# Early first slots of the second attention: projections, row writes and first scores moved ahead, first maxima in another bank, ten throwaway matmuls

## The reference

```python
x = x + linear_attention(layernorm(x))   # causal, 16 heads of 8, elu+1 features
x = x + experts(layernorm(x))            # 16 gated experts, top 4 of 16, and 2 shared
x = x + attention(layernorm(x))          # softmax attention, 16 heads of 8, scale 1/sqrt(8)
x = x + experts(layernorm(x))            # the same expert weights
```

## Time and profile before

| | |
|---|---|
| Runs | 553.9, 556.0, 558.52 us; median 556.0 |
| Profiled execution | 559.11 us, of which 557.4 us are the span of the trace |
| Busy over the span | PE 93%, DVE 73%, ACT 61%, POOL 61% |
| Second attention's first scores | 259.01 us |
| Its second chunk's first scores | 290.60 us |
| Mean granted clock of PE | 0.975 of 2.4 GHz |

### The profile page before, as it was taken

How to read it: one execution, slowest core, us unless ns; L and a number is a source line. 1 busy time by engine, 2 the same in 40 slices (tenths; PEclk the granted TensorE clock), 3 DMA queues, 4 the chain that set the end, 5 groups by cost and what they waited for, 6 DMA issues and landing times.

```text
span 557.4 us, 11771 instructions
## 1 busy us (share of the span) xinstructions
PE 520.1 (93%) x3801; PEld 394.2 (71%) x3801; DVE 407.5 (73%) x1098; ACT 340.4 (61%) x606; POOL 337.9 (61%) x429
## 2 busy tenths in 40 slices
PE   7888989998999999998878989898899999999997
PEld 7666556877888888885545656555578888888885
DVE  4678797676787886676787886978278686686564
ACT  3777766665565556555567675656855655555553
POOL 5897683698767877684613042230488685776663
PEclk9999999999999999999699997969999999999999
DMA  7486870732634233347423344110433444364241
GB/s 178 138 268 192 256 226 5 132 115 67 127 121 127 78 133 92 114 130 246 151 80 102 128 133 125 52 36 2 83 110 110 94 140 123 97 142 131 86 146 38
DMA packets 48566, 67.60 MB, mean 121 GB/s; under 512 B 6641, under 2 KB 18946, under 8 KB 48514
## 3 DMA queue, kind: packets, MB, share of 16 engines
q1 hardware_dynamic: 45408, 66.47, 41.1%
q10 hardware_dynamic: 3106, 0.48, 0.5%
HBM read 53.56 MB, written 13.37 MB: 120 GB/s over the span
## 4 chain that ended last, share of the span: by engine, by line
PE 67%; ACT 11%; DVE 7%; POOL 6%; issue 5%; DMA 3%; SPq 1%; POOLq 0%; DVEq 0%; ACTq 0%
PE bank L1006 15%; PE bank L1008 15%; PE bank L1007 15%; ACT PT L885 6%; PE bank L1128 4%; PE bank L1183 4%; PE bank L1160 2%; DVE PT L1571 2%; POOL KS L745 2%; DMA head_rows<-PHI 2%; PE bank L1013 1%; DVE MEXP L1588 1%; PE bank L1107 1%; PE bank L1071 1%; DMA KS<-head_rows 1%
## 5 line engine op out<-in xcount | busy, mean ns | idle before, releaser
L745 POOL TENSOR_TENSOR KS<-PT,QS 128x512 fp32r<-128x512 f32 x143 | 184.6, 1292 | 85.1 <-ACT QS L981 79.5
L976 ACT ACTIVATE bank<-bank 128x512 f32<-128x512 f32 x128 | 74.6, 582 | 103.5 <-PE bank L1008 102.9
L1685 DVE TENSOR_TENSOR PT<-CS,bank 128x512 f32<-128x512 f32 x128 | 87.6, 684 | 57.6 <-PE bank L1008 56.3
L1006 PE MATMUL bank<-XH,WH 128*128 128x512 f32 (+1 forms) x288 | 114.9, 399 | 0.0
L1008 PE MATMUL bank<-XH,WL 128*128 128x512 f32 (+1 forms) x288 | 112.3, 390 | 0.0
L1007 PE MATMUL bank<-XL,WH 128*128 128x512 f32 (+1 forms) x288 | 112.2, 390 | 0.0
L1588 DVE TENSOR_REDUCE MEXP<-bank 128x4 f32<-128x1024 f32 x64 | 78.3, 1224 | 25.4 <-PE bank L1128 24.5
L1690 DVE TENSOR_TENSOR PT<-PT,bank 128x512 f32<-128x512 f32 x128 | 88.0, 688 | 8.3 <-ACT bank L976 0.3
L981 ACT ACTIVATE QS<-PT 128x512 fp32r<-128x512 f32 x144 | 89.9, 624 | 6.2 <-DVE PT L1690 5.9
L885 ACT ACTIVATE PT<-bank 128x1024 f32<-128x1024 f32 x64 | 65.6, 1026 | 41.3 <-PE bank L1160 41.0
L1183 PE MATMUL bank<-PT,V 128*32 128x256 f32 (+1 forms) x1024 | 65.6, 376 | 0.8 <-ACT OTS L899 0.4
(11 more groups left out here) (208 smaller groups left out, 803.9 us busy)
## 6 DMA issues: line engine op xcount, KB each, us to landing
CS<-combine_rows SPq DMA_DIRECT2D x128, 256.0 KB, 3.2
head_rows<-HP SPq DMA_DIRECT2D x28, 256.0 KB, 3.1
QS<-head_rows SPq DMA_DIRECT2D x28, 256.0 KB, 3.0
KS<-head_rows SPq DMA_DIRECT2D x28, 256.0 KB, 3.7
head_rows<-PHI SPq DMA_DIRECT2D x14, 256.0 KB, 3.7
stage<-in_L_ffn_gate_w_dram SPq DMA_DIRECT2D x5, 192.0 KB, 3.9
stage<-in_L_ffn_up_w_dram SPq DMA_DIRECT2D x5, 192.0 KB, 3.9
stage<-in_L_ffn_down_w_dram SPq DMA_DIRECT2D x5, 192.0 KB, 4.5
```

The lines of the kernel that those rows point to most:

```text
L745: pool.tensor_tensor(GL[:, (u - 1) % 3, :], GG[:, (u - 1) % 3, :], GH[:, (u - 1) % 3, :].bitcast(f32), ALU.subtract).then_inc(F.gl, 1)
L976: act.activation(TH[:, u, :] if u < SHARED else G[u % 3][:, :], G[u % 3][:, :], ACT.Silu).then_inc(F.th, 1)
L1006: pe.matmul(out, wh, vh, start=start, stop=False)
L1685: dve.tensor_tensor(ab, CS[:, e % CBUFS, :], U[u % 3][:, :], ALU.mult).then_inc(F.b, 1)
```

## The change

- **Projections of chunk 0** move from units 6 and 8 to units 0 and 2 of the last chunk of the first expert layer, their ACT copies from units 7 and 9 to 1 and 3, POOL's low halves from 8 and 10 to 2 and 4. The values product stays in unit 10. New waits guard bank 7.
- **Row writes of chunk 0** move on SP from behind the last `CS` load to between the loads 5 to 9 of that chunk, and the read of group 0 behind load 11. Groups 1 to 3 stay behind the last load.
- **Late units**: the downs of units 15 and 16 move from ahead of slot 2 to ahead of slot 3, that of unit 17 from slot 3 to slot 4, the turn and the residual from slot 4 to slot 5, the statistics to slot 6.
- **First maxima** (item 0) are turned into bank 7 (`TP`) and wait for the copies that free it, no longer for the copy of the downs; item 1's turn waits for that now.
- **Throwaways**: 2, 4 and 4 matmuls of the identity by itself, 128 columns, into bank 4, in slots 3, 4 and 5, after the turn of the maxima and ahead of the projection and s1.
- **POOL's low half of chunk 2's norm** (`norm_low`) moves behind the last expert low half.

```diff
+        def maxima_bank(i):
+            return MT if i else TP
...
+        FILLED_SLOTS = {3: 2, 4: 4, 5: 4}
...
-        LATE_UNITS = {2: (0, 1), 3: (2,), 4: (3, 4, 5), 5: (6, 7, 8, 9), 6: (10, 11, 12), 7: (13, 14), 10: (15, 16), 11: (17,)}
+        LATE_UNITS = {3: (0, 1), 4: (2, 3), 5: (4, 5, 6), 6: (7, 8, 9, 10), 7: (11, 12), 8: (13, 14), 10: (15, 16), 11: (17,)}
...
+                    if k == 0 and c == CHUNKS - 1:
+                        if e in (5, 8):
+                            high_rows(0, e // 3 - 1)
+                        if e in (6, 9):
+                            low_rows(0, e // 3 - 2)
+                        if e == 11:
+                            read_rows(0, (0,))
...
             for c in range(CHUNKS):
                 rows(0, c)
-            for c in range(CHUNKS):
+            read_rows(0, range(1, HG))
+            for c in range(1, CHUNKS):
                 spread_rows(c)
...
-                    if u in (8, 10):
-                        rows_low(0, u // 2 - 4)
-                if prev and u == 17 and k == 0:
-                    pool.wait_ge(LN[2].xs, c)
-                    pool.tensor_tensor(ch(XL, c - 1, CHUNK), XS[:, :], ch(XH, c - 1, CHUNK).bitcast(f32),
-                                       ALU.subtract).then_inc(LN[2].xl, 1)
+                    if u in (2, 4):
+                        rows_low(0, u // 2 - 1)
+                if k == 0 and prev and (u == 17 and (more or not cur)):
+                    norm_low(c - 1)
+                if k == 0 and prev and not cur and u == 0:
+                    norm_low(c - 2)
...
-                if k == 0 and cur and prev and not more and u in (7, 9):
-                    biased_rows(0, u // 2 - 3, TP)
+                if k == 0 and cur and prev and not more and u in (1, 3):
+                    biased_rows(0, u // 2, TP)
...
-                    if i:
+                    if i == 0:
+                        pe.wait_ge(LN[2].xs, CHUNKS - 1)
+                    elif i == 1:
+                        pe.wait_ge(FF[0].yt, CHUNKS)
+                    else:
                         pe.wait_ge(A.q2, i)
-                    else:
-                        pe.wait_ge(FF[0].yt, CHUNKS)
                     for t in range(2):
-                        m = pe.transpose(MT[:, P * t:P * (t + 1)], MEXP[:, i % 2, t, :], ident[:, :])
+                        m = pe.transpose(maxima_bank(i)[:, P * t:P * (t + 1)], MEXP[:, i % 2, t, :], ident[:, :])
...
+                    if n in FILLED_SLOTS:
+                        keep_busy(FILLED_SLOTS[n], OT)
...
                 if prev and u == 4:
                     pe.wait_ge(F.yt, c)
+                    if k == 0 and cur and not more:
+                        pe.wait_ge(AT[1].px, 2)
+                    if k == 0 and not cur:
+                        pe.wait_ge(AT[1].q2, 1)
...
-                    if u == 6:
+                    if u == 0:
+                        pe.wait_ge(LN[2].xs, c - 1)
+                    if u in (0, 2):
+                        projection(0, u // 2, TP)
+                    if u == 10:
                         pe.wait_ge(F.res, c)
-                    if u in (6, 8):
-                        projection(0, u // 2 - 3, TP)
-                    if u == 10:
-                        pe.wait_ge(AT[1].px, 2)
                         values(1, 0, TP)
```

More of the change, by code:

```diff
@@ L429, in first_rows, with high_rows, low_rows, read_rows @@
                           .then_inc(A.qr[j], 16)
-            def spread_rows(c):
-                A = AT[1]
[L434 to L438, removed]
+            def high_rows(c, w):
+                sp.wait_ge(AT[1].px, 2 * c + w + 1)
+                write_rows(AT[1], c, w, False)
+            def low_rows(c, w):
+                sp.wait_ge(AT[1].lo, 2 * c + w + 1)
+                write_rows(AT[1], c, w, True)
+            def read_rows(c, groups):
+                A = AT[1]
                 sp.wait_ge(A.qw, 16 * 6 * (c + 1))
-                for j in range(HG):
+                for j in groups:
                     if c:
@@ L448, in spread_rows @@
                           .then_inc(A.qr[j], 16)
+            def spread_rows(c):
+                for w in range(2):
+                    high_rows(c, w)
+                    low_rows(c, w)
+                read_rows(c, range(HG))
             def store(c):
@@ L736, in slot, with norm_low @@
                         route(A, 0, part)
+            def norm_low(c):
+                pool.wait_ge(LN[2].xs, c + 1)
+                pool.tensor_tensor(ch(XL, c, CHUNK), XS[:, :], ch(XH, c, CHUNK).bitcast(f32),
+                                   ALU.subtract).then_inc(LN[2].xl, 1)
             def unit(k, c, u, cur, prev, more):
@@ L1008, in three, with keep_busy @@
                 return pe.matmul(out, wl, vh, start=False, stop=stop)
-            def keep_busy(times):
+            def keep_busy(times, bank=BANK[1]):
                 for _ in range(times):
-                    pe.matmul(BANK[1][:, 0:P], ident[:, :], ident[:, :], start=True, stop=True)
+                    pe.matmul(bank[:, 0:P], ident[:, :], ident[:, :], start=True, stop=True)
             pe.wait_ge(s_id, 2)
@@ L1598, in queries_with_maxima @@
                         dve.wait_ge(A.s2[0], 2 * i - 2)
-                    dve.tensor_tensor(Q2[:, i % 2, :], MT[:, 0:SEQ], QS[:, j, SEQ * b:SEQ * (b + 1)].bitcast(f32),
+                    dve.tensor_tensor(Q2[:, i % 2, :], maxima_bank(i)[:, 0:SEQ], QS[:, j, SEQ * b:SEQ * (b + 1)].bitcast(f32),
                                       ALU.add).then_inc(A.q2, 1)
```

## The result

| | before | changed |
|---|---|---|
| Runs | 12, median 556.78 us (553.44 to 558.52) | 12, median 553.17 us (551.45 to 558.63) |
| Ratio, 95% interval | | 0.995 (0.9928 to 0.9973) |
| Profiled execution | 559.11 us, span 557.4 | 553.41 us, span 551.7 |

The forecast was 553.6 us, within 1% as the likeliest outcome; the time is 553.17, inside the likeliest case's own range.

What follows compares the result with a forecast made beforehand. Bounds: the wait for group 0's keys ahead of the first scores, then a ramp slowed at half clock. First scores -1.3, throwaways +0.8, clock -1.95 sum to -2.4 us: 553.6 us from a median of 556.0, range 549.8 to 557.2.

Steps and rivals of the forecast that it cites:

- likeliest outcome: Whole kernel: a time within 1% (5.6 us) of the kernel before, given a chance of 0.75.
- likeliest case: The prediction's own forecast for the whole kernel, 553.6 us: chance 0.55, own range 552.8 to 554.5 us.
- First scores: Start of the second attention: s0(0) no longer waits for group 0's keys, so less1(0) comes earlier, -1.3 us.
- two conditions: What less1(0) waits for: DVE's maxima, letting it go at 263.7, and group 1's keys, giving 263.7 to 264.1.
- Projections, low halves and row writes: Last chunk of the first expert layer: the moved work hides in existing waits and idle time, cost 0.
- Throwaways: Slots 3 to 5 of the ramp: slot 4's four stand uncovered, +0.8 us; those of slots 3 and 5 cost 0.
- Clock: Ramp, five halves from exp1(0) to exp0(2): throwaways keep the clock from falling to 0.50, -1.95 us.
- Passing on: Behind the ramp each step hangs on the one before, so the whole -2.4 us passes to the end.
- The sum: Whole kernel: -1.3 + 0.8 - 1.95 = -2.4 us, bounds -1.5 to -3.2, taken from a median of 556.0 us.
- The clock falls all the same: Ramp: throwaways do not prevent the fall and cost more, +0.5 us, 556.5 us; chance 0.25.
- Group 1 comes late: Ahead of s0(2): the wait passes to group 1's later read, +2.8 + 0.8, 559.6 us; chance 0.06.
- The fall costs half its length: Ramp: ten fallen microseconds avoided bring 5.0 us back, -5.5 us in all, 550.5 us; chance 0.14.

Runs made afterwards that it cites:

- e8: Changed kernel with the down of unit 15 moved on PE from behind s1(0) to between s0(0) and the projection; 552.26 us.
- e3: Changed kernel with the old order of late units, the old bank for the first maxima and no throwaways; 556.55 us, ratio to the kernel before 1.0005.
- e7: Changed kernel with chunk 0's row writes and the read of group 0 put back behind the last routing load; 559.19 us.
- e6: Changed kernel without the four throwaways of slot 4, those of slots 3 and 5 kept; 552.77 us.
- e10: Changed kernel with e8's moved down and only the four throwaways of slot 5; 553.69 us.
- e9: Changed kernel with e8's moved down and no throwaways in slot 4; 551.97 us, ratio to the kernel before 0.991.
- e1: Changed kernel without its ten throwaways; 555.01 us.
- e11: Changed kernel with e8's moved down and only the two throwaways of slot 3; 554.35 us.
- e4: Changed kernel with the old order of late units and the old bank for the first maxima, throwaways kept; 555.62 us, ratio to the kernel before 1.0004.
- e5: Changed kernel with eight throwaways in slot 4 in place of four; 555.86 us.

## Why the prediction came out

**First scores: right.** s0(0) was to come at 256.2, 0.68 us after the down of unit 14, without a DMA wait; it came after 0.78. The projection was to wait about 0.7 us for unit 17's product and waited 0.61. The term was -1.3, for less1(0) and exp1(0); both came 1.39 earlier. Of its two conditions, group 1 was the later by a little: s0(2) waits 0.25 us for it, and less1(0) follows. e8 moves both forward, since s0(1) and the first turn come earlier too; the wait for group 1 goes away, and less1(0) comes 0.62 us earlier. But the step gave the gain to the early rows and treated the order as a detail of it. e3 and e7 show that neither part carries it alone, and of the 3.49 us ahead of s0(0) only 0.48 had been PE's wait for the keys.

**Projections, low halves and row writes: right.** They were taken at 0. DVE's rows at the head of the result show 38.00 us before and 37.97 now over the last chunk, and no product there waits for a load of routing rows.

**Throwaways: right.** +0.8 for slot 4 and 0 for slots 3 and 5: e6 gives 0.71 over the halves and 0.82 at s0(8). e10 gives no cost for slot 3. Behind slot 5's the exponential at 271.89 starts straight behind ACT's bias copy with no wait for PE, so these lie under ACT's copies.

**Clock: the mechanism right, the term mis-sized.** The step took -1.95, from five halves of 9.9 us without slot 4's cost (9.0 of pace, 0.4 for bias copies, 0.5 for half of a values product). Without slot 4's throwaways (e6, e9) they took 9.3: at full clock the values product (L1102, 273.90 in the first rows) adds nothing (its half took 1.81 us, the steady pace), and the 0.5 charged for it is most of what was too much. Against e1, 11.87 us with the fall, the clock is worth 2.58 us, for 10.2 us at 0.50: 0.25 us for each. e10 and e11 against e9 give 2.72 and 1.94 us at s0(8) for 10.2 and 6.8 us, 0.27 and 0.29 each; the line over all runs says 0.26. These readings agree, so the rival that had half of the fallen time coming back is out. (Two other places give 0.18 and 0.32, see the end.) The rule of the Trainium skill behind it ("TensorE: Matmul & The Clock Gate", Terms: penalty about throttled time times the withheld share of the clock) gives an estimate of 5.1 us for this fall; the measurement decides, and it is half of that, in a loop where ACT and DVE hold PE up part of the time.

**Passing on: nearly.** exp0(2) was to come 2.4 us earlier and came 3.24 earlier, s0(8) only 2.83, so 0.4 was given back in the halves that start at 277.39 and 279.39: they take 2.0 us each, where the loop before took 1.74 to 1.84. DVE's timeline of the changed kernel there:

```profile
277.22 0.18 DVE L1477 BATCH_NORM_AGGREGATE MV<-LNST 128x2 f32<-128x6 f32 x1
...
277.31 0.28 DVE L1477 BATCH_NORM_AGGREGATE MV<-LNST 128x2 f32<-128x6 f32 x3
277.51 1.19 DVE L1627 TENSOR_REDUCE MEXP<-bank 128x4 f32<-128x1024 f32 x1
```

The new table of late units puts the norm's statistics a slot later, and they stand ahead of maxima here; in the kernel before they fell into the slow part of the ramp. I had put them down as hidden in slots with idle. e4 has the old table, and the clock at 1.00 too. The same two halves (ACT's timeline) take 1.74 and 1.97 us there:

```profile
277.42 1.02 ACT L916 ACTIVATE PT<-bank 128x1024 f32<-128x1024 f32 x1 [0.28 <-PE bank L1191]
279.16 1.02 ACT L916 ACTIVATE PT<-bank 128x1024 f32<-128x1024 f32 x1 [0.71 <-PE bank L1191]
281.13 1.02 ACT L916 ACTIVATE PT<-bank 128x1024 f32<-128x1024 f32 x1 [0.95 <-PE bank L1191]
```

So the first of them, some 0.26 us, goes with the table; that it is the statistics among what the table moves is read from the order of the rows, not tried. The second is long with the old table too, and why stays open.

**The sum.** -2.4 was forecast; by the parts it is -1.39 + 0.82 + 0.41 - 2.58 = -2.74, and the two profiles give -2.83 at s0(8). The medians differ by 3.1 to 4.1, the mean times of the twelve runs each by 2.8. Run by run the mean time at 0.50 went from 16.9 to 7.8 us, worth 9.1 x 0.26 = 2.4 us, while at equal clock the kernels differ by 0.4 us (550.2 and 549.8, each with a standard error of 0.1 to 0.2). So the bulk of the gain is the clock; the 1.4 us of earlier scores are mostly paid away again by slot 4 and by these two halves.

That the time came within 0.4 us of the forecast is partly luck. The clock term was 0.63 us too small and the 0.41 that was given back had been put at nothing, so the two errors offset; and the sum was taken from 556.0, the median of three runs. From the 556.8 of twelve it gives 554.4.

**The rivals.** "The clock falls all the same" was nearer than its time says: with fewer throwaways it fell (e10, e11). "Group 1 comes late" did not happen as priced; its wait was there, 0.25 us in the changed kernel and 0.63 in e1, and e8 removed it. "The fall costs half its length" is out by the price above.

## What to carry to other kernels

Cost a moved step together with what stands behind it on the same queue: here the early rows were worth 0.3 us without the order that used them, and the order cost 3.4 us without the rows. Filling matmuls belong only where PE waits anyway: slot 4's, between a release and the scores that ACT waits for, cost 0.18 to 0.23 us each, slot 3's nothing. So try each place alone. Where the clock can fall, compare kernels run by run against the time spent at the lower clock, since one pair of profiles mixes the change with falls elsewhere.

## What the runs showed of the hardware

The price of a fall was 0.25 to 0.29 us for each us at 1.2 GHz in three pairs of profiles of the ramp, and 0.26 over whole runs, in a loop that PE shares with ACT and DVE. It is not the same everywhere. In e5, 6.8 us at 0.50 from 283.6 on put s0(8) 1.26 us further behind exp0(2) than in the changed kernel, 0.18 for each; in e7, where PE had scores and downs one behind the other, 6.8 us went with 2.2 us, 0.32 for each if the clock is all of it.

Busy time alone did not tell where the clock falls. Before and e1 had PE busy for 7.84 and 8.58 us from 257 to 267 and fell at 267 and 266, but in the ten us ahead of its fall e10 had 9.26 (columns of the earlier trace rows):

```profile
253.87:263.87 10.00, 9.26 (x52) 6.11 (x52) 8.63 (x10) 6.35 (x12) 7.60 (x6) 1.00 0.39 124
```

The changed kernel had 9.13 from 257 to 267, and no fall. One execution's fall is also partly chance: the time at 0.50 varies from run to run of the same code. Of 33 runs counted of the kernel before none spent under 7.7 us at 0.50, of the changed kernel two of twelve spent none, and two spent 19 and 26 us. Where PE stood 2.58 us for a transfer (e7) the clock was at 0.50 when it went on, and less1(0) came 4.8 us later than in the changed kernel in all.
